# Four decoder layers on one core: in the first phase, the residual and the second norm moved to right behind the output projection

## What is computed

```python
x = x + L0_xattn(layernorm(x), ctx, mask)     # 16 heads, alibi bias, output projection
x = x + L0_ffn(layernorm(x))                  # shared gated FFN + 2 of 8 experts by a router
x = x + L1_xattn(layernorm(x), ctx)           # inside each token: 16 heads attend to 16 heads
x = x + L1_ffn(layernorm(x))                  # 2 of 8 experts by a router
x = x + L2_xattn(...); x = x + L2_ffn(...)
x = x + L3_xattn(...); x = x + L3_ffn(...)
```

## Time and profile before

| | |
|---|---|
| three runs | 1662.39, 1666.85, 1671.45 us (median 1666.85) |
| the profiled execution's own time | 1666.92 us |
| its span, first to last instruction | 1665.2 us |
| mean granted TensorE clock | 0.875 of full |
| PE, DVE, ACT, POOL busy | 1318.1, 822.9, 443.2, 286.9 us |
| first phase (four groups) | up to about 474 us |

### The profile page before, as it was taken

One profiled execution on the slowest core, in us unless ns is written; L12 is line 12 of the kernel. 1 busy time (PEld: TensorE's weight loads), 2 busy tenths in 40 slices (PEclk: granted clock), 3 DMA queues, 4 the chain that ended last, 5 costly groups with the idle time before them and its releaser, 6 DMA issues. The chain is left out here.

```text
span 1665.2 us, 25790 instructions
## 1 busy us (share of the span) xinstructions
PE 1318.1 (79%) x8177; PEld 1079.1 (65%) x8189; DVE 822.9 (49%) x2295; ACT 443.2 (27%) x1118; POOL 286.9 (17%) x306
## 2 busy tenths in 40 slices
PE   5776586586569777799987877778449999999997
PEld 3553353453447566788855655566349999999996
DVE  3248858858866646112245767575632222222222
ACT  2635235236122223111223232322101111111111
POOL 2010020030010001000124244442311111111111
PEclk9788787687679897899978989888669999999999
DMA  9993040050265474788511001010168888898884
GB/s 340 350 283 97 1 170 28 0 195 3 69 226 179 132 258 141 250 296 296 200 32 39 13 26 51 26 39 0 39 241 306 314 311 312 318 324 314 313 314 156
DMA packets 116317, 291.50 MB, mean 175 GB/s; under 512 B 8193, under 2 KB 90529, under 8 KB 101025
## 3 DMA queue, kind: packets, MB, share of 16 engines
q1 hardware_dynamic: 106032, 273.00, 46.9%
q0 software_dynamic: 10224, 17.77, 4.2%
HBM read 218.84 MB, written 71.90 MB: 175 GB/s over the span
## 5 line engine op out<-in xcount | busy, mean ns | idle before, releaser
L806 PE MATMUL bank<-norm_cols,work 128*128 128x128 f32 x3744 | 470.6, 282 | 35.8 <-ACT norm_cols L1452 18.5
L806 PEld LDWEIGHTS bank<-norm_cols,work 128*128 128x128 f32 x3744 | 459.0, 197 | 52.6 <-issue 38.9
L1697 DVE TENSOR_TENSOR extra<-bank,span 128x256 f32<-128x256 f32 x202 | 85.6, 425 | 392.5 <-ACT span L1494 392.5
L806 PE MATMUL bank<-work,extra 128*128 128x256 f32 x808 | 207.1, 380 | 0.0
L1494 ACT ACTIVATE span<-bank 128x256 f32<-128x256 f32 x202 | 77.4, 383 | 456.3 <-PE bank L806 456.3
L806 PEld LDWEIGHTS bank<-work,extra 128*128 128x128 f32 x808 | 138.6, 191 | 10.7
L2884 POOL DMA_INDIRECT out_x<-att_rows,slot_token x39 | 60.7, 1556 | 377.9 <-ACT att_rows L1504 305.0
L2705 POOL TENSOR_TENSOR rstd<-var_eps,neg_half 128x4 f32<-128x4 f32 x17 | 17.3, 1017 | 550.6 <-DVE var_eps L1709 550.6
L806 PE MATMUL bank<-weights,norm_cols 128*128 128x512 f32 (+1 forms) x192 | 86.8, 600 | 8.3 <-ACT norm_cols L1525 5.5
L806 PE MATMUL bank<-work 128*128 128x256 f32 (+4 forms) x260 | 63.7, 385 | 27.5 <-ACT work L1525 12.3
L905 PE MATMUL bank<-ident,work 128*128 128x128 f32 x256 | 53.7, 370 | 36.7 <-DVE att_rows L1697 27.9
(11 more groups left out here) (348 smaller groups left out, 1980.2 us busy)
## 6 DMA issues: line engine op xcount, KB each, us to landing
work<-in_moe SPq DMA_DIRECT2D x78, 1024.0 KB, 8.0
work<-in_moe SPq DMA_DIRECT2D x39, 2048.0 KB, 8.1
expert_rows_in<-zero SPq DMA_DIRECT2D x3, 5590.0 KB, 47.4
expert_rows_in<-zero SPq DMA_DIRECT2D x3, 5504.0 KB, 36.3
expert_rows_out<-zero SPq DMA_DIRECT2D x3, 5504.0 KB, 22.7
work<-in_moe SPq DMA_DIRECT2D x31, 512.0 KB, 5.7
att_cols<-expert_rows_in SPq DMA_DIRECT2D x39, 130.0 KB, 2.1
att_cols<-expert_rows_in SPq DMA_DIRECT2D x39, 128.0 KB, 3.8
```

Source lines behind the costliest of these rows:

```text
L806: return pe.matmul(o, l, r, start=a, stop=z)
L1697: return dve.tensor_tensor(o, a, b, op)
```

## The change

TensorE: `xT1` and the feed-forward follow `xo` directly; `xT3` and `lg1` go between `down` 0 and `hT` 2; `rk` goes behind `lg`, at the end of the turn. ScalarE follows: it copies `xT3` behind `hT` 1, and its two exponentials for the lists (`router_exps`) go behind the copy of `lg`. VectorE: 8 of the 18 pieces left stay before the add of `xo`, two go into the second norm's wait, three before gate 0, two before gate 1, one before gate 2, `out_stats` before gate 3, `out_rows` behind it; then the first `add_y`, nine pieces of weights, three `add_y`, four of weights and nine of places. POOL computes the second norm's root before layer 1's.

```diff
-    at, mid = k1.index(("xT1", 0)), k1.index(("up", 2))
-    k1f = k1[:at] + l1_keys[0:3] + k1[at:mid] + [("rk",)] + k1[mid:] + [("lg",)]
+    at = k1.index(("hT", 2))
+    k1f = k1[:at] + l1_keys[0:3] + k1[at:] + [("lg",), ("rk",)]
...
                 rows1(plan, turn, "xo", W0["o"], aT)
-                if prev is not None:
-                    layer1_logits(plan, turn, prev)
...
-                        if i == 2 and prev is not None:
-                            list_ranks(plan, turn, prev)
...
                     elif s == "hT":
+                        if i == 2 and prev is not None:
+                            layer1_logits(plan, turn, prev)
...
                 logits(plan, turn, "lg", Wr0)
+                if prev is not None:
+                    list_ranks(plan, turn, prev)
...
                 copy_cols(plan, turn, "aT", aT)
-                if prev is not None:
-                    copy_cols(plan, turn, "xT3", kT)
                 copy_cols(plan, turn, "xT1", xT)
-                if prev is not None:
-                    router_exps(prev)
...
+                    if i == 4 and prev is not None:
+                        copy_cols(plan, turn, "xT3", kT)
...
                 act.activation(LGA[:, ds(g * T * E, T * E)], ps[:, 0:T * E], ACT.Copy).then_inc(bank_empty[b], 1)
+                if prev is not None:
+                    router_exps(prev)
...
-                until("end")
+                some(XO_FRONT)
...
-                norm(lambda t: xg(g, t), lambda t: XN[:, t, :], 1e-5, 2 * g + 2, "normed")
-
-                if prev is not None:
-                    logits_out(plan, turn)
-                    lists(plan, turn, prev, prev, True)
+                norm_stats(lambda t: xg(g, t), 1e-5)
+                some(2)
+                norm_apply(lambda t: xg(g, t), lambda t: XN[:, t, :], 2 * g + 2, "normed")
...
+                some(3)
+                gate(0)
+                some(2)
+                gate(1)
+                until("added")
+                gate(2)
+                some(1)
+                gate(3)
+                until("end")
+                add_y(0)
...
+                if prev is not None:
+                    logits_out(plan, turn)
+                weights(9)
+                for t in range(1, T):
+                    add_y(t)
+                weights(4)
+                places(9)
```

More of the change, by code:

```diff
@@ L149 @@
 L1_FRONT, L1_STEP, L1_SHIFT = 10, 4, 5
+XO_FRONT = 8
 LATE = range(1, T)
@@ L1801, in add_y, with gate @@
                     tt(xg(g, t), xg(g, t), ps[:, 0:D], ALU.add).then_inc(bank_empty[b], 1)
-                for i in range(T):
+                def gate(i):
                     ps, b = full(plan, turn, ("up", i))
@@ L1808, in phase1 @@
                        SG0[:, b, :].rearrange("p (a n) -> p a n", a=2), ALU.mult).then_inc(bank_empty[b], 1)
-                    if i > 1:
-                        add_y(i - 2)
-                add_y(T - 2)
-                add_y(T - 1)
+                some(3)
[8 more added lines that the diff above has]
+                add_y(0)
+                lists_of = None if prev is None else (plan, turn, prev, prev, True)
+                weights, places = (Pieces([] if prev is None else pieces(*lists_of)).some for pieces in (list_weights, list_places))
+                if prev is not None:
[5 more added lines that the diff above has]
+                places(9)
                 for t in reversed(range(T)):
@@ L2015, in layer1_pieces @@
                     own(t, value_products, value_sum)
-                pieces += [divide, add]
+                pieces += [divide, add, "added"]
                 return pieces
@@ L2759, in phase1 @@
                 x_bias(g)
+                power(2 * g + 2)
                 if prev is not None:
                     power(2 * prev + 2, "_l1")
-                power(2 * g + 2)
             def layer1(g):
```

## The result

The changed kernel took 1693.53 us in the median of four executions (1685.78 to 1698.93), against 1666.32 for the four of the kernel before that ran with them: a ratio of 1.016, 95% interval 1.010 to 1.021. It is slower, as forecast, and by 27 us, not 17. Its profiled execution took 1689.56 us with a span of 1687.8, 22.6 more than the span before.

What follows compares the result with a forecast made beforehand. The prediction took group 1's tail to be bound by VectorE and TensorE in turn, with chains of waits in the first phase. Turn ends +6.4 and the last turn +10.6 gave +17.0 on 1666.9: 1684 us, range 1669 to 1694.

Steps and rivals of the forecast that it cites:

- the main mechanism: Context load behind `lg`, scatters on the path, half clock for part or all of the tail; likeliest 1684 us, chance 0.66.
- Step 1: Group 1's tail: `xT1` follows `xo` directly and starts at 200.4 in place of 212.62, 12.2 us earlier.
- Step 2: Layer 1's norm in the tail is 10.4 us later: rows at 215.3, TensorE idle 3.8 us mid feed-forward.
- Step 3: Router's logits in the tail: VectorE reads `lg1` at 223.2, after a new wait of 6 us.
- Step 4: Rest of the feed-forward, half clock for 4.7 us: `lg` ends at 230.5 against 231.62; only 1.1 us left.
- my third rival: The 12 us pass through if norm rows come 3.8 us earlier; `lg` ends 7.6 earlier: 1644 us, chance 0.12.
- Step 5: Turn ends of groups 1 and 2: context load follows `lg`, transposes run cold; 3.2 us each, +6.4 us.
- Step 6: Group 3's turn end: exponentials, lists and scatters behind `lg` make the first expert load 11.7 later, less 1.1: +10.6 us.
- L + 19.7: Group 3's turn end: SyncE's first expert load, counted from the exponential's table load start L; before, L + 8.0.
- the paragraph on what is taken away: Table load moved from behind the first maxima to before the first scores: gain taken as nothing, 1.28 us a turn at most.
- the clock alone, with full speed from `xT3` on: Rival: TensorE keeps full clock through the tail's gap, `lg` ends at 226.8: 1671 us, chance 0.12.

Runs made afterwards that it cites:

- the second, 1695.0: The changed kernel itself, unedited, run again on another occasion: 1695.0 us (1691.0 to 1698.4), ratio 1.016 to the kernel before.
- the fourth experiment: Changed kernel with layer 1's last value sum, division and addition ahead of gate 0, norm statistics behind gate 0, rows behind gate 1: 1680.2 us.
- the first experiment: Changed kernel with SyncE's wait for the next context taken one fill of bank 3 earlier: 1693.2 us.
- experiment 2: Changed kernel with GpSimd's bias on x put ahead of the eight scatters of a turn: 1696.8 us, ratio 1.019.
- experiment 3: Changed kernel with ScalarE's first exponential of the lists, and its table load, ahead of the copy of `hT` 3: 1683.6 us.
- experiment 5: Changed kernel with the context load released one fill of bank 3 earlier and the lists' first exponential ahead of the `hT` 3 copy: 1687.2 us.
- the ninth kernel: The eighth with one unused exponential in group 0's feed-forward, so the loop's turns have no table load at their top: 1656.0 us.
- the eighth: Changed kernel with earlier context, first list exponential and layer 1 norm, bias before scatters, front pieces 8 not 10, two more pieces before last maxima: 1663.0 us.

## Why the forecast came out as it did

The sign and the main mechanism were right, and the size was too small: +17.0 forecast, +22.6 in the profiled execution, +27 in the medians. The first median lies just inside the range (1694) and the second, 1695.0, just outside.

- **Step 1** (12.2 us earlier) holds: `xT1` at 202.62, less the 1.98 by which this turn began later, is 200.6; forecast 200.4.
- **Step 2** holds: norm rows at 215.2 (215.3), `xT3` at 216.6 (216.7), an idle gap of 3.35 (3.8).
- **Step 3** holds: `lg1` is read at 222.9 (223.2), after 6.00 us of idle time.
- **Step 4**: `lg` ended at 229.6, forecast 230.5. The half clock was there, but not for all of the tail: behind the read of `lg1` it lasted 3.9 us where I took 4.7, a part of the 0.9 us by which `lg` came sooner than forecast. The three tails gave 2.0, 1.8 and 0.6, where I took 1.1 each. That nearly nothing of the 12 us would pass through was right; the fourth experiment shows that the order decides it, which my third rival named as its condition.
- **Step 5** holds in size (+4.8 and +4.4 from `lg` to the first maxima, forecast +4.3) and not in its reason. I gave it all to the context load; the first experiment shows a second chain as long, ScalarE's exponentials ahead of the context's copies, and only the two edits together gave the time back. I had looked at bank 4 and not at ScalarE's queue.
- **Step 6** holds: +11.1, forecast +11.7. The scatters are on the path: slots to load is 13.5 us in every version of the new order. By the Trainium skill's price of a switch (ScalarE: Activation LUTs, What ACT_TABLE_LOAD costs), 2.66 us with a drain, L + 19.7 would have been L + 21.1; the trace shows 1.28 with no drain beside it, and L + 19.05, so row and page differ on the drain and the row holds.
- **The step that failed** is the paragraph on what is taken away, "VectorE's pieces between the maxima set the pace there, so I give it nothing": it leaves those stretches as they were. For the moved table load the sentence holds (1 to 2 is 3.45 us in group 1 before and after), but no sentence asks what stands on GpSimd behind the scatters, which the later lists hold back. The stretches between the maxima took 4.4 and 2.3 us more. The bias on GpSimd, which the change never touches, slid from VectorE's wait onto its products (2 us a turn, experiments 2, 3 and 5). The rest is TensorE's clock, 2.4 us in group 2 and 0.4 in group 3; in experiment 2 it is there without the bias, and its cause is open. The Trainium skill has the rule (SBUF — State Buffer, SBUF: two separate sides): a VectorE operation with two inputs in SBUF and a GpSimd operation that reads SBUF take turns on a shared pair of SBUF ports, whichever starts first holds the pair for its whole instruction, and the other stands still. The trace agrees that one stands still for the whole of the other (3.52 us for 0.69 beside a bias of 2.36), and not on which: VectorE's record begins 0.6 us before the bias's, and VectorE is the one held.
- **Missed as well**: where the table load of a turn would be paid. The prediction has it ahead of the first scores and looks for its price at the maxima. It stands at the top of the turn, ahead of ScalarE's copies of the context, for which the keys wait: 1.0 us in group 1 (20.07 to 21.08), and in the other turns hidden behind the context until the context came early.
- **Not forecast, and not the change's**: TensorE's clock in group 1's maxima, 2.7 us between two executions of the same kernel. The two profiled executions differ by 8.8 us in all: 2.7 here, 1.3 in the tail behind it, and the rest almost wholly in the first and the last row of the table.

That the clock alone, with full speed from `xT3` on, would have given 1671 us was not tried apart from the order: in the fourth kernel the gap went, and with it two thirds of the half clock.

## What to carry to other kernels

When a step is moved behind another, follow every queue behind it: here the lists took with them the norm of the next turn, eight scatters and a bias on GpSimd, and ScalarE's copies. If removing one wait gains nothing, look for a second chain of the same length before calling the wait free; the two edits that each left a turn's start at 25 us cut 4 us from it together. And look where the gain lands: here those 4 us moved the products back onto the bias, and the time of the whole kernel did not fall. Work freed on one engine is only worth what the order of the other lets through: ask where the producer idles just ahead of the wait (4.12 us here), and move the pieces into that.

## What the runs showed of the hardware

- A GpSimd addition of 128x1024 takes 2.35 us whatever runs beside it; VectorE's operation beside it goes on until the addition has ended, and 0.2 to 0.8 us more: 0.69 to 3.52, 0.96 to 3.67, 0.42 to 2.38, 1.38 to 3.45 (four operations from SBUF to SBUF). In the first two VectorE's had begun 0.6 and 0.5 us earlier by the records. A reduction that reads PSUM is not held up: 1.29 with and without.
- A table load of 1.28 us on ScalarE can cost more than its length through TensorE's clock: in the ninth kernel, behind an idle gap of 0.92 us, the keys ran at 2.4 GHz (granted clock 1.00 over 3.7 us), in the eighth, behind 2.00 us, at 1.2 for a good part (0.55 over 3.4 us). The short gap does not assure it: in the kernel before, group 1's keys came behind 0.92 us at 0.52 over their first 3.4.
- The clock's return differs between two executions of the same program at the same place: over six us of group 1's maxima the granted clock was 1.00 in one and 0.50 in another, 2.7 us of time.
